# Four fused transformer layers on one core: the first loads reordered and spread between contexts, four tiles' roots moved to VectorE, twelve products of ones put ahead

## The reference

```
def _layernorm(x, axis=-1, eps=1e-05):
    m = jnp.mean(x, axis=axis, keepdims=True)
    v = jnp.var(x, axis=axis, keepdims=True)
    return (x - m) / jnp.sqrt(v + eps)
...
q = (x @ Wq).reshape(B, N, NUM_HEADS, HEAD_DIM).transpose(0, 2, 1, 3)
k = (context @ Wk).reshape(B, M, NUM_HEADS, HEAD_DIM).transpose(0, 2, 1, 3)
v = (context @ Wv).reshape(B, M, NUM_HEADS, HEAD_DIM).transpose(0, 2, 1, 3)
attn = jax.nn.softmax(jnp.einsum('bhnd,bhmd->bhnm', q, k) * scale, axis=-1)
out = jnp.einsum('bhnm,bhmd->bhnd', attn, v)
...
return out @ Wo + bo
...
x = x + _L0_xattn_ref(_layernorm(x, axis=-1), ctx_1024, L0_xattn_Wq, L0_xattn_Wk, L0_xattn_Wv, L0_xattn_Wo, L0_xattn_bo)
x = x + _L0_ffn_ref(_layernorm(x, axis=-1), ...)
```

## Time and profile before

| | |
|---|---|
| median of 3 runs | 1381.38 us (1377.89 to 1383.59) |
| profiled execution, its own time | 1384.29 us |
| its span in the trace | 1382.5 us |
| busy: PE, DVE, ACT, POOL | 1206.2, 1004.0, 891.2, 582.2 us |
| `l0x` before its steady pace | the scores of batch 2 begin at 43.34 us |
| then per batch | about 8.0 us |

### The profile page before, as it was taken

How to read it: one execution, slowest core, us unless ns; L and a number is a source line. 1 busy time by engine, 2 the same in 40 slices (tenths; PEclk the granted TensorE clock), 3 DMA queues, 4 the chain that set the end, 5 groups by cost and what they waited for, 6 DMA issues and landing times.

```text
span 1382.5 us, 30489 instructions
## 1 busy us (share of the span) xinstructions
PE 1206.2 (87%) x9899; PEld 941.1 (68%) x9942; DVE 1004.0 (73%) x2234; ACT 891.2 (64%) x2419; POOL 582.2 (42%) x680
## 2 busy tenths in 40 slices
PE   3899889999988999997989999987999998997824
PEld 2677677777766788885777777765788765666513
DVE  3666677766677899996667765586666786887687
ACT  2666456655564799995777776764566546775584
POOL 5800266666653222263221342340777516882100
PEclk9999999999999999998999999999999999998967
DMA  8000000000001556640000010000422017660001
GB/s 287 13 9 8 17 2 2 0 0 0 0 2 58 191 211 208 215 174 1 2 0 1 1 42 0 0 1 28 150 85 95 0 31 184 185 163 1 1 0 31
DMA packets 37446, 82.98 MB, mean 60 GB/s; under 512 B 5074, under 2 KB 18514, under 8 KB 37236
## 3 DMA queue, kind: packets, MB, share of 16 engines
q1 hardware_dynamic: 37364, 81.94, 19.0%
HBM read 80.27 MB, written 1.64 MB: 59 GB/s over the span
## 4 chain that ended last, share of the span: by engine, by line
PE 59%; ACT 16%; DVE 12%; issue 7%; SPq 2%; POOL 2%; DMA 1%; ACTq 0%; DVEq 0%; POOLq 0%
PE score_bank L1600 16%; ACT h_all L1052 11%; PE score_bank L1461 6%; PE f_bank L1634 6%; PE f_bank L1378 5%; PE turn_bank L1477 4%; PE out_bank L1517 3%; PE turn_bank L1634 3%; PE out_bank L1634 3%; PE out_bank L1486 3%; SPq L564 2%; PE score_bank L1452 2%; DVE top_score L1941 1%; PE f_bank L1401 1%; PE out_bank L1526 1%
## 5 line engine op out<-in xcount | busy, mean ns | idle before, releaser
L1052 ACT ACTIVATE h_all<-score_bank,top_score 128x128 f32<-128x128 f32 x896 | 282.7, 402 | 118.7 <-DVE top_score L1941 118.6
L1600 PE MATMUL score_bank<-parts 128*128 128x512 f32 x1040 | 296.8, 403 | 12.1 <-DVE h_parts L2150 8.5
L1600 PEld LDWEIGHTS score_bank<-parts 128*128 128x128 f32 x1040 | 193.2, 191 | 77.0 <-DVE h_parts L2150 19.0
L1941 DVE TENSOR_REDUCE top_score<-score_bank 128x4 f32<-128x512 f32 x224 | 143.0, 681 | 133.2 <-PE score_bank L1461 133.2
L2150 DVE TENSOR_TENSOR h_parts<-score_bank,h_parts 128x512 fp32r<-128x512 f32 x260 | 178.2, 685 | 2.5 <-ACT h_parts L1167 2.2
L1167 ACT ACTIVATE h_parts<-score_bank 128x512 fp32r<-128x512 f32 x260 | 155.8, 599 | 33.5 <-DVE score_bank L2134 8.7
L1477 PE MATMUL turn_bank<-CF,h_all 128*128 128x128 f32 x512 | 82.0, 283 | 40.7 <-DVE work L1953 22.8
L746 POOL TENSOR_TENSOR small<-small,half_neg 128x4 f32<-128x4 f32 (+4 forms) x25 | 37.7, 1510 | 183.2 <-DVE small L1914 86.5
L1477 PEld LDWEIGHTS turn_bank<-CF,h_all 128*128 128x128 f32 x512 | 55.4, 142 | 67.2 <-ACT h_all L1052 22.0
L771 POOL TENSOR_TENSOR h_all<-h_all,prob_rec 128x512 f32<-128x512 f32 x64 | 66.6, 1049 | 70.5 <-DVE prob_rec L1945 70.3
L1461 PEld LDWEIGHTS score_bank<-work 32*128 32x128 f32 (+1 forms) x2304 | 78.9, 189 | 22.9 <-issue 22.1
(11 more groups left out here) (405 smaller groups left out, 2789.2 us busy)
## 6 DMA issues: line engine op xcount, KB each, us to landing
work<-gates_l0m SPq DMA_DIRECT2D x62, 512.0 KB, 4.0
W0X<-gates_l2m SPq DMA_DIRECT2D x32, 256.0 KB, 3.9
CTX<-gates_l2m SPq DMA_DIRECT2D x32, 256.0 KB, 3.8
wset<-in_l0m SPq DMA_DIRECT2D x32, 128.5 KB, 3.6
W0X<-gates_l1m SPq DMA_DIRECT2D x8, 512.0 KB, 3.8
wset<-in_l1m SPq DMA_DIRECT2D x8, 384.0 KB, 4.5
CTX<-gates_l1m SPq DMA_DIRECT2D x6, 512.0 KB, 3.8
big<-in_w0f SPq DMA_DIRECT2D x4, 512.0 KB, 8.0
```

Of the source, the lines that this page charges most:

```text
L1052: last = act.activation(held[c][:, P * m:P * m + P], score_bank[c][:, P * m:P * m + P], ACT.Exp, bias=top_score[c][:, m:m + 1], **sums)
L1600: last = pe_.matmul(bk[:, :], wt, y[:, x], start=(part == 0), stop=(part == len(parts_of) - 1))
L1941: dve.tensor_reduce(top_score[c][:, :], split(score_bank[c][:, :], HEADS), AX_X, ALU.max, negate=True)\
```

## The change

SP's list is reordered: only the first four tiles, the constants, the contexts of batches 0 and 1 and the first three parts of `W0X` go ahead; the fourth part, with two small rows, has a semaphore of its own (`in_w0o`). All other transfers become `pieces`, one behind the context of each of batches 2 to 12, and the contexts' loop is written out. VectorE measures four tiles, computes their roots itself by a bit shift, an integer step and four Newton steps, normalises two tiles, and measures the other twelve ahead of step 0; GpSimd's power is left for tiles 4 to 15. GpSimd fills its constants first, `ones_bf` before all, and TensorE multiplies it by itself twelve times while the loads run. ScalarE's sine moves from behind step 0 to behind step 2. The diff, cut:

```diff
-            load(X[:, 0:4, :], a["x"][0:4].rearrange("b s d -> s b d"), in_x)
-            load(X[:, 4:B, :], a["x"][4:B].rearrange("b s d -> s b d"), in_x)
+            load(X[:, 0:4, :], a["x"][0:4].rearrange("b s d -> s b d"), in_x4)
             load(CF[:, :], a["cf"], in_c)
             load(VEC[:, :], a["vec"], in_c)
             load(BROW[:, :], a["brow"], in_c)
-            load(BOX[:, :], rows_to_all(a["brow"][:, 0:P]), in_c)
...
-            with sp.Fori(1, PAIRS) as i:
-                for s in range(2):
-                    for job in (2, 3):
-                        r, k = place(front_at["l0x"], 4, i - 1, s, job)
-                        sp.wait_ge(f_full[r], k + 1)
-                    context0(i, s)
+            context0(0, 0)
+            load(W0X[:, 0:3, :], split(a["w0x"][:, 0:3 * BANK], 3), in_w0x)
+            context0(0, 1)
+            load(X[:, 4:B, :], a["x"][4:B].rearrange("b s d -> s b d"), in_x)
+            load(BOX[:, :], rows_to_all(a["brow"][:, 0:P]), in_x)
+            load(W0X[:, 3, :], a["w0x"][:, 3 * BANK:4 * BANK], in_w0o)
+            load(ROWS[:, 0:2 * P], rows_to_all(a["rows"]), in_w0o)
+            load(GCOL[:, :], a["rows"][:, 0:P].rearrange("o p -> p o"), in_w0o)
+            pieces = {2: lambda: weights0("qa"), 3: lambda: weights0("ka"), 4: lambda: weights0("v"), 5: lambda: weights0("o")}
...
+            pieces[6], pieces[7], pieces[8] = shared, routers, places
+            pieces[9] = lambda: load(CTX[:, :, :], a["ctx"].rearrange("b s d -> s b d"), in_w1)
...
+            for b in range(2, B):
+                for job in (2, 3):
+                    r, k = place(front_at["l0x"], 4, b // 2 - 1, b % 2, job)
+                    sp.wait_ge(f_full[r], k + 1)
+                context0(b // 2, b % 2)
+                if b in pieces:
+                    pieces[b]()
...
+            pool.memset(ones_bf[:, :], 1.0).then_inc(step("setup.warm"), 1)
             link(pool.memset(waited[:, :], 0.0))
-            power("l0x")
...
+            power("l0x", 1)
+            pool.wait_ge(in_x4, 16)
             pool.wait_ge(in_x, 16 * 2)
...
-            pool.wait_ge(in_rows, 16 * 15)
+            pool.wait_ge(in_w0o, 16 * 3)
...
+            pool.wait_ge(in_rows, 16 * 13)
...
-            two_layers(act, "ACT", "l0x", attention(LAYERS[0]), "l0f", attention(LAYERS[1]), after={("l0x", 0): sines})
+            two_layers(act, "ACT", "l0x", attention(LAYERS[0]), "l0f", attention(LAYERS[1]), after={("l0x", 2): sines})
...
-            pe_.wait_ge(in_c, 16 * 4)
-            pe_.wait_ge(in_w0x, 16)
+            pe_.wait_ge(step("setup.warm"), 1)
+            for _ in range(12):
+                pe_.matmul(out_bank[:, :], ones_bf[:, :], ones_bf[:, :].unsqueeze(1).to_broadcast([P, 4, P]), start=True, stop=True)
+            pe_.wait_ge(in_c, 16 * 3)
...
-            dve.wait_ge(in_x, 16 * 2)
-            for b in range(B):
+            dve.wait_ge(in_x4, 16)
+            for b in range(4):
                 measure(X, b)
             variances("l0x", 0)
-            variances("l0x", 1)
+            x, y, t = ve[:, 0:4], r1[:, 0:4], t0[:, 0:4]
+            dve.wait_ge(varied, 1)
+            link(dve.tensor_scalar(y.bitcast(I32), x.bitcast(I32), 1, None, ALU.logical_shift_right))
+            link(dve.tensor_scalar(y.bitcast(I32), y.bitcast(I32), -1, 0x5f3759df, ALU.mult, ALU.add))
+            for n in range(4):
+                link(dve.tensor_tensor(t, y, y, ALU.mult))
+                link(dve.scalar_tensor_tensor(t, t, -0.5, x, ALU.mult, ALU.mult))
+                last = dve.scalar_tensor_tensor(y, t, 1.5, y, ALU.add, ALU.mult)
+                if n < 3:
+                    link(last)
+            last.then_inc(rooted, 1)
             powered("l0x", 0)
+            def later_tokens():
+                dve.wait_ge(in_x, 16 * 2)
+                for b in range(4, B):
+                    measure(X, b)
+                variances("l0x", 1)
...
-                       ahead={("l0x", B - 2): lambda: variances("l0f", 0), ("l0f", B - 1): lambda: variances("l0m", 0),
+                       ahead={("l0x", 0): later_tokens, ("l0x", 2): lambda: powered("l0x", 1),
```

More of the change, by code:

```diff
@@ L358, in build @@
         in_bias, csum_made = sem("in_bias"), sem("csum_made")
+        in_x4, in_w0o = sem("in_x4"), sem("in_w0o")
         recip_ready = pair("recip_ready")
@@ L570, in _, with weights0 @@
             load(BROW[:, :], a["brow"], in_c)
-            load(BOX[:, :], rows_to_all(a["brow"][:, 0:P]), in_c)
             def context0(i, s):
                 sp.dma_start(cT[s][:, :], a["ctxT"][bass.ds(2 * i + s, 1), :, :].rearrange("o p n -> (o p) n")).then_inc(cT_ready[s], 16)
-            for s in range(2):
[L577 to L592, removed]
+            def weights0(n):
+                at = {"qa": 0, "ka": 2, "v": 4, "o": 5}[n]
                 load(w0f[n], a["w0f"][:, 1024 * at:1024 * at + 1024], in_w0f)
@@ new lines, in shared, with routers @@
+            def shared():
+                load(CB[:, :], a["cb"], in_rows)
+                load(BOX1[:, :], rows_to_all(a["brow"][:, 2 * P:3 * P]), in_rows)
+                load(CROW[:, :], rows_to_all(a["brow"][:, P:2 * P]), in_rows)
+            def routers():
+                load(RB[:, :], rows_to_all(a["l0m_rb"]), in_rows)
+                load(LB[:, :], rows_to_all(a["l2m_bias"]), in_rows)
+                for g in range(CHUNKS):
+                    load(B2[32 * g:32 * g + 32, :], a["b2"], in_rows)
+                load(RW[:, 0:39], a["rw"], in_rows)
+                load(RWB[:, :], a["rwb"], in_rows)
@@ new lines, in places @@
+            def places():
+                load(POSI[:, :], rows_to_all(a["pos"]), in_rows)
+                load(MASKU[:, :], rows_to_all(a["mask"]), in_rows)
+            pieces[6], pieces[7], pieces[8] = shared, routers, places
+            pieces[9] = lambda: load(CTX[:, :, :], a["ctx"].rearrange("b s d -> s b d"), in_w1)
+            pieces[10] = lambda: load(W1X[:, :], a["w1x"], in_w1)
+            pieces[11] = lambda: load(W1F[:, :], a["w1f"], in_w1)
+            pieces[12] = lambda: load(WL2[:, :], a["wl2"], in_w1)
@@ L742, in power @@
                         continue
+                    if name == "l0x":
+                        pool.wait_ge(rooted, 1)
                     pool.wait_ge(varied, part_at[name] + part + 1)
@@ L872, in _ @@
             pool.memset(GATES[:, :, 31:32], 1.0).then_inc(step("setup.ones"), 1)
+            power("l0x", 1)
+            pool.wait_ge(in_x4, 16)
             pool.wait_ge(in_x, 16 * 2)
-            pool.wait_ge(in_c, 16 * 4)
+            pool.wait_ge(in_c, 16 * 3)
             pool.tensor_tensor(AO[:, :, :], X[:, :, :], over(BOX[:, :], B), ALU.add).then_inc(skip_ready, 1)
@@ L1395, in front_job @@
                         if u == 2:
+                            if isinstance(i, int) and 2 * i + s == 0:
+                                pe_.wait_ge(in_w0x, 16)
                             pe_.wait_ge(cT_ready[t], 16 * (s // 2 + 1) + 16 * i)
@@ L1523, in unit_step @@
                         pe_.wait_ge(gathered, B + 2 * s + 2 + 4 * i if n == "l0f" else s + 1 + 2 * i)
+                        if n == "l0x" and isinstance(i, int) and 2 * i + s == 0:
+                            pe_.wait_ge(in_w0o, 16 * 3)
                         count, w = (4, W0X[:, 3, :]) if n == "l0x" else (8, w0f["o"])
@@ L1992, in do @@
                             dve.wait_ge(step("setup.tables"), 1)
-                            dve.wait_ge(in_rows, 16 * 15)
+                            dve.wait_ge(in_rows, 16 * 13)
                             powered(n, 0)
@@ L2211, in _ @@
             two_layers(dve, "DVE", "l0x", attention(LAYERS[0]), "l0f", attention(LAYERS[1]),
-                       ahead={("l0x", B - 2): lambda: variances("l0f", 0), ("l0f", B - 1): lambda: variances("l0m", 0),
+                       ahead={("l0x", 0): later_tokens, ("l0x", 2): lambda: powered("l0x", 1),
+                              ("l0x", B - 2): lambda: variances("l0f", 0), ("l0f", B - 1): lambda: variances("l0m", 0),
                               ("l0f", B): lambda: normalise("l0m", AO, False, range(3))},
-                       after={("l0x", 0): lambda: powered("l0x", 1), ("l0x", B + 1): lambda: variances("l0f", 1),
+                       after={("l0x", B + 1): lambda: variances("l0f", 1),
                               ("l0f", 2): tokens_places})
```

5 lines of the change are left out of this document (2 added, 3 removed).

## The result

The changed kernel took 1372.29 us (median of 8 runs, 1369.48 to 1373.85), the kernel before 1378.4 on the same chip (8 runs, 1374.77 to 1383.59). The ratio is 0.9952, interval 0.9934 to 0.9971: 6.1 us won, where 6.0 was forecast; the interval stands for 4.0 to 9.1 us. The profiled execution took 1370.87 us, its span is 1369.1.

A forecast was written before the change was run, and what follows sets the result against it. Bound: a chain of waits through the first batches, with SP's issue and a queued context, then an engine pipeline. Terms 7.6 + 3.9 - 3.7 - 3.3 + 1.5 - 0.5, plus 0.5, gave 6.0 us won: 1375.5, range 1369 to 1380.5.

The forecast's parts named there:

- The start: Ahead of batch 0: four tiles land early and VectorE makes their roots, `y_tok` at 8.2 instead of 15.83; 7.6 us won.
- The context of batch 2: Between batches 1 and 2: its transfer no longer waits behind the full queue, 11.9 us become 8.0; 3.9 us won.
- The sine's new place: In front of the steady loop: two table loads and the sine show, plus one microsecond of lower clock; 3.7 us lost.
- The load in the loop: First in ScalarE's loop body: a table load repeated in four more passes, 0.83 us each; 3.3 us lost.
- The mask: GpSimd's conversion moves behind batch 8's context and meets VectorE's division in about 4 cases of 10; 1.5 us won.
- `AO`: Its making on GpSimd now runs beside batch 0's divisions on VectorE; 0.5 us lost, bounds 0 and 2.
- The products: Twelve early TensorE products: higher clock taken as lost again by the keys; 0.5 us won for the chance it partly holds.
- Rival B: TensorE's higher clock is kept up to batch 0's first keys, 2.7 us lower: 1373, chance 0.17.
- C: In the loop, the repeated table load costs nothing or is hidden, 3.3 us less: 1372, chance 0.13.
- E: Contexts wait behind the pieces in the queue, about 8 us each, 16 in all: 1391, chance 0.06.
- D: The start wins less: `W0X` or `AO` late, mask meets division again, together 2 to 4 us: 1378.5, chance 0.14.

The follow-up runs named there:

- the run with one load: Changed kernel plus one exponential activation behind the sine, so the exponentials' table is loaded before the loop: 1366.15 us, ratio 0.9901 against the kernel before.
- the run with GpSimd's power: Changed kernel with the first four tiles' roots made by GpSimd's power, VectorE's fourteen instructions left out: 1380.24 us, ratio 1.0009 against the kernel before.
- the early sine with the split: Changed kernel with GpSimd's angles first, sine behind step -1, `AO` and mask conversion in four instructions each: 1374.78 us, ratio 0.9976 against the kernel before.

## Why the prediction was right

The gain and its sign came out as forecast, 6.1 us for 6.0. The time itself, 1372.29, lies 3.2 below the 1375.5 that was stated, because the forecast started from the median of three runs, 1381.38, and eight runs of the kernel before gave 1378.4. The closeness of the gain is partly luck: the terms missed by up to 0.5 us each and largely cancelled, and the 1.6 us behind `l0x`'s last scores stood in no term.

- **The start, 7.6.** `y_tok` came at 8.42 (8.2 forecast), the keys at 9.72 (9.5), the scores at 16.20 (16.0): 7.4 measured. The roots went from 5.66 to 8.38, 2.7 us for fourteen, where 2.8 was taken. `W0X` did not hold the keys: they waited for `yT`. The prediction took the roots as one link of the chain; the run with GpSimd's power showed that they carry the whole term.
- **The context of batch 2, 3.9.** Measured 3.9, and shown by taking it away: 9.1 us.
- **The sine's new place, 3.7 lost.** Measured 3.2, from one profile (3.7 with one load, where that batch took 11.74). The clock did fall (the products with `yT` at 46.16 took 1.89 instead of 1.06), and by the total it cost half of the one microsecond taken.
- **The load in the loop, 3.3 lost.** 3.4 by the pass (0.86 for 0.83), and the run with one load took it back.
- **The mask, 1.5 won.** 1.4 measured, though not for the reason given. The conversion did meet the division again (1.98), and a `y_tok` met GpSimd's weights and took 2.43 instead of 0.34, a collision that the prediction did not name and that now stands in the chain of waits. Both together cost 1.3, the one meeting of before 2.7. Most of the difference is the clock. In the kernel before TensorE had stood 2.21 us for VectorE, which was held by the division (up to 66.11), and the granted clock was 0.51 for 67 to 69 us, where the products with the values stand:

```profile
67.96 1.98 PE L1517 MATMUL out_bank<-work,V 128*64 128x128 f32 x16
```

The scores behind took 1.42. In the changed kernel TensorE had stood 1.56, the clock stayed at 1.00, and the same products took 1.09 (76.49) and 1.16, together 1.2 us less.

- **`AO`, 0.5 lost.** The division waited (1.93), and batch 1 to 2 took 7.97, so it was hidden: about 0. In the run with one load, where the clock rose sooner, it waited 4.09 and batch 1 to 2 took 8.59: 0.6.
- **The products, 0.5 won in part.** Nothing in the profiled execution, and by the eight profiles an estimated 0.4 on the mean. Rival B, which named 2.7 us, is what two of the eight show (first scores 3.0 earlier than in the changed kernel's profile, 1.7 earlier than in most); as the usual case it is refuted. The sign named for it, first scores that take 1.16, doesn't tell it: they took 1.16 in seven of the eight profiles and without any product too. What tells it is the keys (1.16 instead of 2.07).

Of the rivals, C is refuted by the extra activation, E by the chain (no transfer of a context in it; `cT` landed in 1.8), and D's parts by the keys at 9.72, except that the mask did meet the division.

## What to carry to other kernels

When a chain at the head of a kernel is shortened, find out for each link whether its input or its engine held it: GpSimd's arithmetic was not to be had before 10.8 us whatever its data, and moving fourteen small instructions to VectorE, 2.7 us of work, won 7.4 together with the small transfer. A function of another table that stands right ahead of a loop puts a load into each of its passes; one dummy activation behind it held ScalarE for 0.1 us (42.90 to 43.01) and won 6.1 here, 3.4 of it by its loads. And a long instruction of GpSimd beside VectorE's chain kept VectorE waiting less in four pieces, even though its own time grew; the times alone don't show that gain.

## What the runs showed of the hardware

- GpSimd's first instruction that isn't a memset started 10.8 to 15.6 us into the program, 8.6 to 12.7 after its list came to it, in the five kernels in which it waited for no data (the latest with the early sine and the split); the power behind it started at once. Why is open.
- Loading the activation table that is already there took 1.28 us, as long as a switch.
- Where VectorE's division began at the same moment as GpSimd's conversion of the mask (70.17 in the run with one load), the division took 0.69 and the conversion 2.44 instead of 1.89: the wait can fall on GpSimd as well. Where the conversion had begun first (71.72 in the changed kernel), the division waited (1.98).
- The clock column read 1.00 up to its first change, whatever the clock was. In the kernel before it reads 1.00 for 23.6 to 26.0 while the scores took 2.08, and without products it reads 1.00 for 9 to 12 while the keys took 2.08. In the changed kernel it has fallen to 0.50 at 9 us, and agrees with the keys' 2.07. Up to the first change the durations have to be read and not the column.
